# Clearing the edge mask at other steps, and scaling the second layer's weights in halves, in a two-layer graph attention kernel

## The reference

```python
def transformer_conv(x, src, dst, Wq, bq, Wk, bk, Wv, bv, Ws, bs, H, C, concat):
    q, k, v = ((x @ W + b).reshape(n, H, C) for W, b in ((Wq, bq), (Wk, bk), (Wv, bv)))
    alpha = einsum('ehc,ehc->eh', q[dst], k[src]) / sqrt(C)
    p = exp(alpha - segment_max(alpha, dst)[dst])
    out = segment_sum(p[:, :, None] * v[src], dst) / segment_sum(p, dst)[:, :, None]
    out = out.reshape(n, H * C) if concat else out.mean(axis=1)
    return out + x @ Ws + bs
h = relu(transformer_conv(x, ..., H=4, concat=True))
out = transformer_conv(h, ..., H=2, concat=False)
return layernorm(x + out)
```

## Time and profile before

| | us |
|---|---|
| median of 3 runs | 1829.64 |
| the profiled execution | 1829.15 |
| its span | 1827.3 |
| TensorE busy in the span | 1732.7 (95%) |
| VectorE busy | 1555.2 (85%) |
| ScalarE busy | 1259.5 (69%) |
| GpSimd busy | 1169.5 (64%) |

### The profile page before, as it was taken

How to read it: one execution, slowest core, us unless ns; L and a number is a source line. 1 busy time by engine, 2 the same in 40 slices (tenths; PEclk the granted TensorE clock), 3 DMA queues, 4 the chain that set the end, 5 groups by cost and what they waited for, 6 DMA issues and landing times. The chain is left out here.

```text
span 1827.3 us, 45046 instructions
## 1 busy us (share of the span) xinstructions
PE 1732.7 (95%) x15000; PEld 1301.8 (71%) x15000; DVE 1555.2 (85%) x4541; ACT 1259.5 (69%) x2093; POOL 1169.5 (64%) x1461
## 2 busy tenths in 40 slices
PE   3779799999999999999999999989899999999997
PEld 2556567777777777777777777756677777677775
DVE  7999888988888898888888888835788888988886
ACT  4579877777777777777777777732566676666675
POOL 4200057787877777777767777733577777777776
PEclk9899999999999999999999999999999999999999
DMA  6779857777778777778777887692599999989995
GB/s 163 227 201 259 236 120 158 156 154 154 154 159 161 159 156 153 155 164 157 159 153 153 161 162 155 127 233 54 106 174 185 174 185 177 172 176 184 172 188 108
DMA packets 753664, 301.76 MB, mean 165 GB/s; under 512 B 655863, under 2 KB 734075, under 8 KB 750184
## 3 DMA queue, kind: packets, MB, share of 16 engines
q1 hardware_dynamic: 752266, 296.96, 78.2%
q0 software_dynamic: 640, 1.63, 0.3%
q10 hardware_dynamic: 528, 0.26, 0.0%
HBM read 93.63 MB, written 47.83 MB: 77 GB/s over the span
## 5 line engine op out<-in xcount | busy, mean ns | idle before, releaser
L1429 POOL TENSOR_TENSOR prob_parts_l<-prob_l,prob_parts_l 125x512 f16<-125x512 f32 x600 | 720.5, 1231 | 13.6 <-ACT prob_parts_l L1544 13.6
L1535 ACT ACTIVATE prob_l<-prob_l,neg_max_l 125x1024 f32<-125x1024 f32 (+1 forms) x450 | 521.2, 1160 | 2.1 <-DVE neg_max_l L1630 1.8
L1836 PE MATMUL score_l<-room,QT_l 128*128 128x512 f16 (+2 forms) x2100 | 512.7, 354 | 1.4 <-DVE scale_rows L1802 1.2
L1550 ACT CAST probT_l<-transposed_l 128x375 f16<-128x375 f32 x450 | 213.0, 473 | 410.0 <-PE transposed_l L1862 410.0
L1877 PE MATMUL output_l<-V,prob_flipped_l 128*128 128x256 f16 x2400 | 459.6, 272 | 1.3 <-DMA prob_flipped_l<-prob_parts_l 1.3
L1879 PE MATMUL output_l<-V,prob_flipped_l 128*128 128x128 f16 x2400 | 427.5, 219 | 0.0
L1622 DVE CUSTOM_DVE_ANT_0 prob_l<-score_l,mask_even 125x512 f32<-125x512 f32 (+2 forms) x546 | 332.7, 614 | 85.8 <-PE score_l L1836 84.2
L1622 DVE CUSTOM_DVE_ANT_0 prob_l<-score_l,mask_odd 125x512 f32<-125x512 f32 (+2 forms) x504 | 307.9, 614 | 78.0 <-PE score_l L1836 76.3
L1544 ACT CAST prob_parts_l<-prob_l 125x1024 f16<-125x1024 f32 x300 | 309.4, 1033 | 0.1
L1877 PE MATMUL output_l<-V,probT_l 128*128 128x256 f16 x1350 | 272.0, 273 | 2.7 <-DVE probT_l L1635 1.9
L1877 PEld LDWEIGHTS output_l<-V,prob_flipped_l 128*128 128x128 f16 x2400 | 233.7, 97 | 52.2 <-issue 1.9
(11 more groups left out here) (217 smaller groups left out, 2375.4 us busy)
## 6 DMA issues: line engine op xcount, KB each, us to landing
mask_scratch<-log SPq DMA_DIRECT2D x87, 420.0 KB
mask_even<-mask_scratch SPq DMA_DIRECT2D x25, 448.0 KB
mask_odd<-mask_scratch SPq DMA_DIRECT2D x24, 448.0 KB
mask_odd<-mask_scratch SPq DMA_DIRECT2D x12, 896.0 KB
mask_even<-mask_scratch SPq DMA_DIRECT2D x12, 896.0 KB
prob_flipped_l<-prob_parts_l SPq DMA_TRANSPOSE x600, 3.1
hT_scratch<-rowsT_l SPq DMA_DIRECT2D x24, 250.0 KB, 3.6
mask_odd<-mask_scratch SPq DMA_DIRECT2D x12, 471.2 KB
```

What stands on the lines that cost most here:

```text
L1429: pool.tensor_tensor(parts[0:TP, 1, a:b], prob[:, h % 2, a:b], parts[0:TP, 0, a:b], ALU.subtract).then_inc(s_flo, 1)
L1535: act.activation(e, e, ACT.Exp, bias=neg_max[:, h % 2:h % 2 + 1], accum_out=total[:, h % 2, c:c + 1]).then_inc(s_exp, 1)
L1550: act.copy(probT[:, q, 0, 0:n, 0:TP], flipped_in_psum(h, q, n)).then_inc(s_hi, 1)
L1836: last = pe.matmul(score_bank(h, p)[:, 0:b - a], QT[:, h % 2, i, :], KT[:, h, j, a:b], start=n == 0, stop=n == len(PRODUCTS) - 1)
```

## The change

In layer 1 the clearing steps are set anew. Before: piece 0 at (0, 2), 1 at (0, 5), 2 at (1, 2), 3 at (1, 5), 4 at (2, 1), 5 at (2, 4), 6 at (2, 6), all for the next tile. Now: piece 2 at (0, 3), 3 at (1, 4), 4 at (2, 1), 5 at (2, 3), 6 at (2, 6) for the next tile, and pieces 0 and 1 at (3, 2) and (3, 5) for the tile after the next. Tile 1's pieces 0 and 1 are cleared at (0, 1) and (0, 2) of tile 0. The number of clearings and their order by piece stay as they were.

The second layer's weight matrices are scaled in six halves: `weights_scaled` in head 2's step and `weights_back` in head 3's, of tiles 3 to 8.

```diff
-        CLEAR_AT = ({(0, 2): 0, (0, 5): 1, (1, 2): 2, (1, 5): 3, (2, 1): 4, (2, 4): 5, (2, 6): 6} if layer == 1 else
+        CLEAR_AT = ({(0, 3): 2, (1, 4): 3, (2, 1): 4, (2, 3): 5, (2, 6): 6, (3, 2): 0, (3, 5): 1} if layer == 1 else
-        CLEAR_AHEAD = {p: 2 if layer == 2 and p in PART_PIECES[0] else 1 for p in range(NP)}
+        CLEAR_AHEAD = {p: 2 if p in PART_PIECES[0] else 1 for p in range(NP)}
...
-                def weights_scaled(i):
-                    w = second["W"][i]
+                def weights_scaled(n):
+                    i, ks = (0, 2, 1)[n // 2], slice(n % 2 * H1 // 2, (n % 2 + 1) * H1 // 2)
+                    w = second["W"][i][:, ks, :]
...
-                        if layer == 1 and h == 1 and 3 <= t <= 5:
-                            weights_scaled((0, 2, 1)[t - 3])
-                        if layer == 1 and h == 2 and 3 <= t <= 5:
-                            weights_back(t - 3, (0, 2, 1)[t - 3])
+                        if layer == 1 and h == 2 and 3 <= t <= 8:
+                            weights_scaled(t - 3)
+                        if layer == 1 and h == 3 and 3 <= t <= 8:
+                            weights_back(t - 3)
...
-                    act.wait_ge(s_scaled2, 6)
+                    act.wait_ge(s_scaled2, 12)
...
+                            if layer == 1 and is_first(t) and (h, k) in ((0, 1), (0, 2)):
+                                clear_mask(1, k - 1)
```

More of the change, by code:

```diff
@@ L1451, in finish, with weights_back @@
                                            ALU.add).then_inc(s_out, 1)
-                def weights_scaled(i):
-                    w = second["W"][i]
+                def weights_scaled(n):
+                    i, ks = (0, 2, 1)[n // 2], slice(n % 2 * H1 // 2, (n % 2 + 1) * H1 // 2)
+                    w = second["W"][i][:, ks, :]
                     pool.wait_ge(s_chain2, STEPS2)
-                    pool.tensor_tensor(w, w, rows2[:, i, :].unsqueeze(1).broadcast_to([C, H1, H2 * C]), ALU.mult).then_inc(s_scaled2, 1)
-                def weights_back(n, i):
-                    w = second["W"][i]
+                    pool.tensor_tensor(w, w, rows2[:, i, :].unsqueeze(1).broadcast_to([C, H1 // 2, H2 * C]), ALU.mult).then_inc(s_scaled2, 1)
+                def weights_back(n):
+                    i, ks = (0, 2, 1)[n // 2], slice(n % 2 * H1 // 2, (n % 2 + 1) * H1 // 2)
+                    w = second["W"][i][:, ks, :]
                     pool.wait_ge(s_scaled2, 2 * n + 1)
-                    pool.tensor_tensor(w, w, second["h_back"][:, :].unsqueeze(2).broadcast_to([C, H1, H2 * C]), ALU.mult
+                    pool.tensor_tensor(w, w, second["h_back"][:, ks].unsqueeze(2).broadcast_to([C, H1 // 2, H2 * C]), ALU.mult
                                        ).then_inc(s_scaled2, 1)
```

## The result

The changed kernel takes 1834.61 us (median of 6 runs, 1830.09 to 1838.72), the kernel before 1829.83 (6 runs, 1827.92 to 1830.43). The ratio is 1.0023, interval [1.0012, 1.0033]: slower by 4.2 us, between 2.2 and 6.0. The prediction was +1.6 us and a range up to 1833.2, so it was wrong: the loss is more than twice as large, and outside the range (the medians alone are 4.8 us apart). The profiled execution has a span of 1831.1 us against 1827.3.

A forecast was written before the change was run, and what follows sets the result against it. The prediction took TensorE to bound the kernel in the tiles touched. Its terms, 1.8 (tiles 1 and 2) + 0.3 (tiles 10 to 12) - 0.5 (halves) = +1.6 us, gave a median of 1831.2 us, range 1828.9 to 1833.2.

The forecast's parts named there:

- What bounds the kernel: Layer 1's tiles: TensorE sets the pace, busy 770.00 of 770.00 us from 410 to 1180 us.
- the margins: Start of a head: VectorE's masked score comes 0.79 us, its low part 0.49 us, before TensorE needs them (tile 9).
- a usual tile at 0: Head 3's new clearings, 0.68 and 1.40 us, fall into VectorE's waits and the margins: cost 0 a tile.
- tile 0 at 0: Two clearings at (0, 1) and (0, 2): the extra 0.7 us ends in a wait; 0, at most 0.3.
- the loads in time: Mask parts arrive before their moved clearings, piece 0's some 4 us early, and no queue is passed.
- Rival (b): Every tile stands still at its start: +4.6 to +11.5 us on top of the sum, 1836 to 1843; chance 0.08.
- Tiles 1 and 2, +1.8 us: Head 3: new clearings beside the scale chain delay masked scores; TensorE stands still 0.9 us a tile, between 0.55 and 1.3.
- the dearer branch: At (3, 5) of tile 1, clearing and chain step both wait for GpSimd, so the clearing adds its 1.4 us.
- the two branches: At (3, 5) of tile 1: clearing adds 1.4 us if both wait, 0.65 if it takes over the step's waiting.
- Tiles 10 to 12, +0.3 us: Head 3, with `weights_low` of 1.22 us at (3, 3): load 3.30 against room 2.58 us; 0.1 a tile.
- The halves, -0.5 us: Halved scalings fit GpSimd's wait for the next query, removing tile 3's standstill of 0.41 us; between 0 and -0.6.
- The range: Whole kernel: 1828.9 to 1833.2 us, the upper end from tiles 1 and 2, tiles 10 to 12 and spread.

The follow-up runs named there:

- e3: The changed kernel with one clearing one step later, piece 2 at (0, 4) instead of (0, 3): 1831.93 us, ratio 1.0007.
- e4: The changed kernel with each weights_back half moved behind the sums of head 3, in head 0 of the tile after: 1831.78 us, ratio 1.0015.
- e2: The changed kernel with the clearings back at their steps of before, so the halves alone: 1830.91 us, ratio 0.9999 against the kernel before.
- e1: The changed kernel with the weights scaled whole in tiles 3 to 5 as before, so the new clearings alone: 1836.96 us, ratio 1.0036.
- e7: The changed kernel with the halves in heads 1 and 2 of tiles 3 to 8, where the whole scalings were: 1834.22 us, ratio 1.0019.
- e8: The kernel before with one number changed, piece 3 cleared at (1, 4) instead of (1, 5): 1835.17 us, ratio 1.0031.

## Why the prediction was wrong

The forecast was 1.8 + 0.3 - 0.5 = +1.6 us; by the tile periods these terms came to 1.75, 0.0 and +2.51. By its own steps:

- *What bounds the kernel, the margins, a usual tile at 0, tile 0 at 0, the loads in time*: right. Tiles 9 to 23 of the changed kernel run at 38.71 us, with clearings of 0.68 to 0.81 at (3, 2) and mostly 1.44 at (3, 5), and no wait of VectorE for a mask part shows. Head 0 of tile 0, with the two extra clearings, takes 9.75 us against 9.72. Rival (b), a standstill in every tile, did not come.
- *Tiles 1 and 2, +1.8 us*: right in mechanism and size. Measured 1.01 + 1.13 - 0.39 = +1.75. Both instructions waited, as in the dearer branch, which gave 1.3 us a tile; the 0.82 and 0.93 measured lie near its middle value of 0.9. In tile 1 the clearing and the step added 1.04 + 0.10 = 1.14 us, between the 0.65 and the 1.4 of the two branches; in tile 2 they added more, 1.42 + 0.15, and short gaps took up more than the 0.2 that was allowed for them. That the middle fits so well is in part luck.
- *Tiles 10 to 12, +0.3 us*: measured 0.0, as the prediction held possible. The clearing at (3, 5) took only 1.0 us in these tiles, where 1.40 was put in.
- *The halves, -0.5 us*: wrong, and this step made the miss. Measured +2.51 us in tiles 3 to 8 (3.09 of loss, less the 0.58 of tile 3 before). The sentence that failed is that "both halves fit in such a wait", the wait for the next query. In GpSimd's queue the sums of the head (`finish`) stand between the low parts and that query, so they were behind the new instruction too; and in head 3 their last one feeds TensorE's transposes at (0, 4). The prediction asked who waits behind the half and looked at the last in the queue, not at each. Second, its sum took the lock as a cost to VectorE alone. The clearing moved to (0, 3) met L1440 and made GpSimd the loser, 0.6 us to 1.16. Third, the clearing at (3, 5) held the low parts ahead of the half up by 0.45 us, which the prediction weighed for a usual tile only. e3 and e4 show that the half's place and the collision at (0, 3) are not enough without each other; e2 takes away the clearings at (0, 3) and (3, 5) together. Each of the three changes takes the loss of these tiles to 0, but for 0.27 in tile 5 of e4. Tile 5 of the changed kernel has a DMA wait in it whose cause is open.
- What the halves were priced against was also mis-read. The 0.41 us of tile 3 did go (e2: 0 in tile 3). But e1 shows that with the new clearings the whole scalings would have cost 1.6 to 2.7 us a tile in three tiles. Beside that the halves are a gain, 8.17 to 5.23 us. In tiles 3 to 8 neither the clearings nor the halves have a cost of their own that could be added to the other's.
- *The range*: its upper end held tiles 1 and 2 high and gave the halves' term an end of 0 and no more. A term for an instruction that comes into a queue ahead of work that TensorE waits for should have had an upper end of its own: 1.03 us of the half and 0.5 of the collision, less the margin, in six tiles.

The rule quoted from the Trainium skill, page "SBUF — State Buffer", section "Who interferes with whom", is borne out by e7 and e8: a clearing that began behind a GpSimd instruction ended 0.42 us behind the end of that instruction, whether this was one of 1.27 or of 2.37 us. The rule speaks of both sides; the prediction's sum used it for one.

## What to carry to other kernels

When an instruction is put into an engine's queue, go through every instruction behind it up to the first real wait, and for each ask who waits for its result; the wait that hides it must lie ahead of the first of these, not behind the last. Where two engines share a port, moving an instruction to a cheap place also moves the other engine's next instruction, and with long instructions on one side and short critical ones on the other the order of arrival decides, here a clearing's lead of 0.07 us, turned into a lag of 0.19, cost 1.8 us a tile. Below 1% of the time, compare the period of one tile across traces: here it told 0.1 us apart, where ten runs of the total tell some 2 us.

## What the runs showed of the hardware

VectorE's clearing, with both inputs in SBUF, waits for a GpSimd instruction that began before it until that one ends: 2.60 us behind one of 2.37 us that had begun 0.19 ahead, 1.30 behind one of 1.27 begun 0.39 ahead, 0.55 where it came first. It works the other way too: 1.16 instead of 0.6 us for GpSimd's scaling of 128 columns beside a clearing of 0.68. When VectorE had two such instructions in a row in the midst of GpSimd's low parts, both were long (1.04 us instead of 0.68, and 1.25 where steps of the same size take 0.28 to 0.41), and GpSimd's four low parts took 5.07 us instead of the 4.56 of the kernel before: the two engines took turns, and VectorE did not keep its own between its two instructions.
